# Gates travelling with the rows, result weighting on GpSimd and accumulating gathers in an attention and mixture-of-experts kernel

## The chip, the cores and the metric

The kernel runs on one core of one Trainium2 chip. A core has TensorE (PE; its weight loads are PEld), VectorE (DVE), ScalarE (ACT), GpSimd (POOL) and SyncE (SP), which here only issues DMAs. The metric is the device time of one execution in microseconds (us); lower is better. Each engine works through its own queue in order and waits on semaphores.

## The reference

One layer of a parallel block on x of 32 samples x 256 tokens x 128 features, all float32, cut to what matters:

```python
xn = layernorm(x)
# attention: 16 heads of 64; the first 32 dims of q and k are rotated
q, k, v = xn @ W_qkv;  q, k = rope(q), rope(k)
attn = softmax(causal(q @ k.T) / 8);  a = (attn @ v) @ W_o
# experts: 8 and a ninth that hands its input through, top 2 of 9 by softmax
probs = softmax(xn @ router_w + router_b)
gates = the two largest probs, else 0
y[e] = gelu(xn @ w1[e]) @ w2[e]              # w1: 128x512, w2: 512x128
out = x + a + sum_e gates[e] * y[e] + gates[8] * xn
```

Only the rows that chose an expert are sent through it. Matmuls split float32 into fp16 high and low parts and run three products (`split3`).

## The kernel before, in words

`acc` in SBUF holds x as 64 tiles of 128 tokens and becomes the output. After a prologue (normalisation, transposes, router, and slots: the place of each token's two rows in a list sorted by expert) come three stages.

**Former samples** (0 to 15) and **latter samples** (16 to 31) run the attention, one sample after the other, each in eight *periods* p, one for two heads of the 16. All loops are unrolled in Python, and each engine has its own `sample(b, parity, at)` that writes its queue by hand. Per period, VectorE does: `turned` (some evictions of transposed probabilities), `rest_low`, `masks` (L956: scores plus mask, and row maxima), `turn` (L918, L919: products with cosine and sine of a projected unit), `o_scale` (L983), `invert` in even periods (L966 to L972: reciprocals of the softmax sums in two fp16 parts), `rope_low` (L930), `mix` in period 0 (L907), `combine` in latter samples (L897), `y_add`. TensorE does: `scores` (L1173), `turn_sums` (L1195: the inverses brought into the layout of the outputs; it waits for `inv_parts` of the period before), the projection units of the period (L1102 to L1104), `transposes` (L1184), `attend` (L1211, L1212). ScalarE evicts, does the exponentials (L643), `rest_high` (L587), `v_copy` (L599) and `o_copy` (L633), which takes one of two `o_whole` buffers that GpSimd's `o_split` (L474, L476) frees. GpSimd does `o_split`, `q_rope_low` (L481), `rope_add` (L456, L457) and one indirect DMA a period.

Which unit is projected in which period is laid down by `USUAL`, `AHEAD` and `VALUES`, and `plan` sorts them: within a period `rest` comes last, and in period 6 `v_low`. Units share two PSUM banks in turn.

In former samples GpSimd's `send` (L497) scatters a normalised tile of 128 rows, 512 bytes each, from `stage` to its slots in `sorted_x` in DRAM, twice, for the two choices. `normalise_row` (L488) makes the tile every second period. Each send waits for the landing of the one before (semaphore `sent`):

```python
pool.wait_ge(send_ready, tile + 1)
pool.wait_ge(sent, 16 * (TOP * tile + n))
nc.gpsimd.indirect_dma_start(out=sorted_x, ...in_=stage[:, i, :]...).then_inc(sent, 16)
```

**The experts** stage takes 72 tiles of 256 sorted rows: SP loads (L383) four ahead, TensorE transposes (L1248), computes hidden and down products, ScalarE does gelu (L709), `h_hi` (L714) and the output copy into `ys` (L698), VectorE the fp16 splits (L1062, L1072, L1076), and SP stores to `sorted_y` (L401). GpSimd has nothing to do.

In **latter samples** GpSimd's `gather` (L507) fetches 128 result rows to one of four `stage` buffers, eight a sample (the two tiles of a former sample and the two of this one, two choices each). `combine` (L897) multiplies them by the gate of each token and adds them to `acc`. SP stores finished tiles, and in all samples but the last of a half it copies the parts of q and k into `q_stack` and `k_stack` (L326, four DMAs each, `stack_q` and `stack_k`).

## Time and profile before

| | |
|---|---|
| median of 3 runs | 1500.76 us (1494.09 to 1503.2) |
| profiled execution, time | 1500.74 us |
| profiled execution, span | 1499.0 us |
| busy TensorE / VectorE / ScalarE / GpSimd | 84% / 80% / 75% / 57% |
| mean granted TensorE clock | 0.965 |

The span runs from the first to the last instruction of the profiled execution. Busy shares are means over stages with different limits, so they say little by themselves. In the rows further down, "idle before" and the wait table give the time that an engine stood still and what ended it; L numbers are lines of the kernel.

### The profile page before, as it was taken

Reading aid. Unit: us, or ns where it says so; the run is one execution under the profiler, and the core shown is the slowest. Engines: PE = TensorE matmul, PEld = TensorE weight load, DVE = VectorE, ACT = ScalarE, POOL = GpSimd, SP = SyncE. Lnnn points to the kernel's source line nnn. Section 1 sums busy time; section 2 is a strip of 40 time slices with the busy share of each in tenths; the row PEclk is TensorE's granted clock in tenths of the full one; section 3 lists DMA queues with packets and bytes.
Section 4 is the critical chain, followed back from the end, with each engine's and each line's share of the span. In section 5 each row is a group of like instructions: output and inputs, shape, how many; then the busy total and the mean of one; then the engine's idle time right before and its main releaser. Section 6 shows DMA issues by size and latency. Waiting matters only on the chain.

```text
span 1499.0 us, 46446 instructions
## 1 busy us (share of the span) xinstructions
PE 1254.0 (84%) x15156; PEld 940.5 (63%) x15157; DVE 1195.7 (80%) x4018; ACT 1122.6 (75%) x3606; POOL 858.6 (57%) x1194
## 2 busy tenths in 40 slices
PE   1416999888888898895999999888888889888888
PEld 1404666666666666664889898566666666666666
DVE  5788877777777887783777777889988889889886
ACT  6415888877787787784878887878777777777786
POOL 3254777777777777773000000767777777666775
PEclk9757999999999999997999999999999999999999
DMA  9621433333333333333232322333333333333330
GB/s 290 204 56 38 101 73 73 74 72 72 74 72 74 72 80 79 75 83 111 72 88 84 87 84 75 77 80 79 80 82 92 91 84 80 89 91 89 85 80 27
DMA packets 115831, 130.12 MB, mean 87 GB/s; under 512 B 11568, under 2 KB 75312, under 8 KB 115376
## 3 DMA queue, kind: packets, MB, share of 16 engines
q1 hardware_dynamic: 107056, 110.26, 30.6%
q0 software_dynamic: 8576, 17.33, 3.8%
q8 instruction: 110, 1.80, 0.5%
q14 instruction: 89, 0.73, 0.2%
HBM read 28.85 MB, written 31.59 MB: 40 GB/s over the span
## 4 chain that ended last, share of the span: by engine, by line
PE 28%; DVE 22%; DMA 17%; POOL 16%; issue 13%; ACT 4%; POOLq 0%; DVEq 0%; SPq 0%; ACTq 0%
DMA sorted_x_dram<-stage,slots 17%; PE bank L1102 6%; PE bank L1103 6%; PE bank L1104 6%; DVE arena L956 4%; POOL sorted_x_dram L497 3%; POOL arena L476 3%; PE bank L1173 3%; DVE arena L919 2%; DVE arena L918 2%; POOL arena L456 2%; PE bank L1184 2%; POOL arena L457 2%; ACT probs L643 2%; PE bank L1211 2%
## 5 line engine op out<-in xcount | busy, mean ns | idle before, releaser
L643 ACT ACTIVATE probs<-arena,neg_max 128x128 f32<-128x128 f32 (+1 forms) x1024 | 452.3, 446 | 110.5 <-DVE neg_max L956 108.5
L956 DVE CUSTOM_DVE_ANT_0 arena<-bank,causal 128x128 f32<-128x128 f32 (+1 forms) x1024 | 302.3, 349 | 46.6 <-PE bank L1173 46.1
L507 POOL DMA_INDIRECT stage<-sorted_y_dram,slots x128 | 130.5, 1020 | 257.9 <-DVE arena L919 238.6
L1184 PE MATMUL bank<-ident,probs 128*128 128x128 f32 x1536 | 212.6, 275 | 13.5 <-ACT probsT L626 10.7
L633 ACT ACTIVATE o_whole<-bank 128x256 f32<-128x256 f32 x256 | 97.7, 382 | 151.5 <-PE bank L1195 85.2
L497 POOL DMA_INDIRECT sorted_x_dram<-stage,slots x128 | 133.3, 1041 | 128.6 <-DMA sorted_x_dram<-stage,slots 104.2
L1184 PEld LDWEIGHTS bank<-ident,probs 128*128 128x128 f32 x1536 | 177.2, 142 | 39.6 <-issue 18.4
L643 ACT ACTIVATION_READ_ACCUMULATOR probs<-arena,neg_max 128x1 f32 x1024 | 194.7, 190 | 0.0
L1102 PE MATMUL bank<-arena 128*128 (+1 forms) x864 | 183.2, 238 | 1.5 <-DVE arena L1076 1.5
L476 POOL TENSOR_TENSOR arena<-o_whole,arena 128x256 f16<-128x256 f32 x256 | 172.0, 672 | 21.0
L1103 PE MATMUL bank<-arena 128*128 (+1 forms) x864 | 182.7, 238 | 0.0
L1173 PE MATMUL bank<-arena 64*128 64x128 f16 (+1 forms) x3072 | 172.1, 245 | 12.1 <-DVE neg_max L956 9.8
L1104 PE MATMUL bank<-arena 128*128 (+1 forms) x864 | 178.8, 237 | 0.0
L626 ACT ACTIVATE probsT<-bank 128x384 f32<-128x384 f32 x384 | 170.3, 479 | 2.1
L1195 PE MATMUL bank<-ident_h,inv_parts 128*64 128x128 f16 x2048 | 106.3, 226 | 76.8 <-DVE inv_parts L972 76.5
L1211 PE MATMUL bank<-probsT,arena 128*64 128x256 f32 x1024 | 169.6, 406 | 0.0
L1102 PE MATMUL bank<-xnT_lo,wqk_hi 128*128 128x256 f16 x512 | 142.9, 279 | 27.5 <-DVE arena L924 19.8
L456 POOL TENSOR_TENSOR arena<-arena 128x256 f32<-128x256 f32 x128 | 94.1, 735 | 103.4 <-DVE arena L919 100.7
L1195 PEld LDWEIGHTS bank<-ident_h,inv_parts 128*64 128x64 f16 x2048 | 65.4, 109 | 135.2 <-DVE inv_parts L972 99.6
L924 DVE SCALAR_TENSOR_TENSOR arena<-bank,arena 128x512 f16<-128x512 f32 x128 | 87.5, 685 | 76.4 <-ACT arena L587 76.2
L1104 PE MATMUL bank<-xnT_hi,wqk_hi 128*128 128x256 f16 x512 | 141.3, 276 | 0.0
L1103 PE MATMUL bank<-xnT_hi,wqk_lo 128*128 128x256 f16 x512 | 141.3, 276 | 0.0
(152 smaller groups left out, 3258.8 us busy)
## 6 DMA issues: line engine op xcount, KB each, us to landing
arena<-arena SPq DMA_DIRECT2D x256, 256.0 KB, 3.8
arena<-sorted_x_dram SPq DMA_DIRECT2D x72, 128.0 KB, 2.2
sorted_y_dram<-stage SPq DMA_DIRECT2D x72, 128.0 KB, 1.8
sorted_x_dram<-arena SPq DMA_DIRECT2D x3, 2304.0 KB, 17.8
arena<-experts_dram SPq DMA_DIRECT2D x8, 512.0 KB, 5.6
out_dram<-acc SPq DMA_DIRECT2D x32, 128.0 KB
sorted_x_dram<-arena SPq DMA_DIRECT2D x1, 2368.0 KB, 19.1
sorted_x_dram<-stage,slots POOLq DMA_INDIRECT x128, 2.5
```

The lines of the kernel that those rows point to most:

```text
L476: nc.gpsimd.tensor_tensor(lo, o_whole[:, j % 2, :], hi, ALU.subtract).then_inc(o_done, 1)
L497: nc.gpsimd.indirect_dma_start(out=sorted_x, out_offset=bass.IndirectOffsetOnAxis(ap=slots[:, tile, n:n + 1], axis=0), in_=stage[:, i, :], ...
L626: nc.scalar.activation(probsT[:, s % 4, :], TP[s % 2][:, 0:PW], ACT.Copy).then_inc(t_out[1], 1)
L643: last = nc.scalar.activation(probs[:, s % 4, at:at + w], masked[:, s % 4, at:at + w], ACT.Exp, bias=neg_max[:, s % 4, t:t + 1], scale=-1. ...
L956: last = nc.vector.tensor_tensor_reduce(out=masked[:, (s + i) % 4, at:at + w], in0=SC[i][:, at:at + w], in1=causal[:, at:at + w], scale=1. ...
L1102: mm(dst, a_hi, b_lo, start=start, stop=False)
L1103: mm(dst, a_lo, b_hi, start=False, stop=False)
L1104: return mm(dst, a_hi, b_hi, start=False, stop=stop)
L1173: last = mm(SC[h][:, at:at + w], q_stack[parity][rows, r, ql, u, qs], k_stack[parity][rows, r, kl, u, 0:w], start=(n == 0), stop=(n == 2))
L1184: last = nc.tensor.transpose(TP[s % 2][:, k * P:(k + 1) * P], probs[:, s % 4, k * P:(k + 1) * P], ident[:])
L1195: last = mm(INV[j % 2][64 * i:64 * i + 64, t * P:(t + 1) * P], of, ident_h[:], start=(l == 0), stop=(l == 1))
L1211: mm(PV[j % 2][rows, :], v_sb[:, 0, vs], probsT[:, s % 4, 0:SEQ], start=True, stop=False)
```

## The change

- Rows in DRAM are 129 words wide (`sent_rows`). The last word is the gate of the row for this choice. `stage` holds 2 tiles in place of 4; `normalise_row` therefore waits for the sends of two tiles earlier. GpSimd writes the gate's column before each send.
- In the experts stage GpSimd takes the gate column out of each loaded tile (`keep_gates`) and multiplies the results in `ys` by it (`gate`), before SP stores them. `ys` has buffers of its own. SP's store waits for `gated`.
- Gathers add into `acc` directly (`compute_op=ALU.add`), first both tiles with choice 0, then both with choice 1, each second one waiting for the first of its tile. `combine` is gone from VectorE.
- `o_whole` has three buffers (`OUTPUTS`).
- VectorE's `invert` stands directly behind `masks`.
- In `plan`, units that belong to a sample further ahead come first within a period; nothing is put last any more. In effect `rest` 0 comes before `y` 1 in period 5 and `rest` 1 before `v_low` 1 in period 7.
- ScalarE waits for the last stores of the experts ahead of the first `rest` of the latter samples, since `ys` now lies where the parts of q are.

```diff
+ROW = D + 1
+SENDS = 2
+OUTPUTS = 3
...
-    steps = [(p, kind, j, b if kind == "v_high" else b - 1 if kind == "y" else b + 1)
-             for p, kind, j in (OPENERS if b in (0, MID) else USUAL) if nearer or kind in ("v_high", "y")]
-    steps += [(p, kind, j, b + 2) for p, kind, j in AHEAD if further]
+    opening = b in (0, MID)
+    steps = [(p, kind, j, b + 2) for p, kind, j in AHEAD if further]
+    steps += [(p, kind, j, b if kind == "v_high" else b - 1 if kind == "y" else b + 1)
+              for p, kind, j in (OPENERS if opening else USUAL) if nearer or kind in ("v_high", "y")]
     steps += [(p, kind, j, b + 1) for p, kind, j in VALUES if nearer]
-    return sorted(steps, key=lambda step: (step[0], step[1] == "rest" or step[0] == 6 and step[1] == "v_low"))
+    return sorted(steps, key=lambda step: step[0])
...
-        stage = sb("stage", [P, BACKS, D], F32)
+        stage = sb("stage", [P, SENDS, ROW], F32)
...
-        ys = [stage[:, 2 * i:2 * i + 2, :] for i in range(2)]
+        gate_rows = sb("gate_rows", [P, BODY, 2], F32)
+        ys = [view(PART + i * 256, 256).rearrange("p (k d) -> p k d", d=D) for i in range(2)]
...
                     if not last:
                         sp.wait_ge(xs_ready, i + 1)
+                        sp.wait_ge(gates_kept, i + 1)
                         load(i + BODY, k)
-                    sp.wait_ge(y2_done, i + 1)
+                    sp.wait_ge(gated, i + 1)
...
                 tile = PER * b + i
-                if tile >= PER:
-                    pool.wait_ge(sent, 16 * TOP * (tile - PER + 1))
-                nc.gpsimd.tensor_scalar(stage[:, i, :], acc[:, tile, :], neg_mean[:, tile:tile + 1], rstd[:, tile:tile + 1],
-                                        ALU.add, ALU.mult).then_inc(send_ready, 1)
+                if tile >= SENDS:
+                    pool.wait_ge(sent, 16 * TOP * (tile - SENDS + 1))
+                nc.gpsimd.tensor_scalar(stage[:, i % SENDS, 0:D], acc[:, tile, :], neg_mean[:, tile:tile + 1], rstd[:, tile:tile + 1],
+                                        ALU.add, ALU.mult).then_inc(normalised, 1)
+                nc.gpsimd.tensor_copy(stage[:, i % SENDS, D:ROW], gates[:, tile, 0:1]).then_inc(send_ready, 1)
 
             def send(b, k):
 
                 i, n = k // TOP, k % TOP
                 tile = PER * b + i
-                pool.wait_ge(send_ready, tile + 1)
                 pool.wait_ge(sent, 16 * (TOP * tile + n))
+                if n > 0:
+                    nc.gpsimd.tensor_copy(stage[:, i % SENDS, D:ROW], gates[:, tile, n:n + 1]).then_inc(send_ready, 1)
+                pool.wait_ge(send_ready, TOP * tile + n + 1)
+                pool.wait_ge(normalised, tile + 1)
                 nc.gpsimd.indirect_dma_start(
...
+            def keep_gates(i, k):
+
+                pool.wait_ge(xs_in[k], 4 * (i - k) + 16)
+                if i >= BODY:
+                    pool.wait_ge(gated, i - BODY + 1)
+                nc.gpsimd.tensor_copy(gate_rows[:, k, :], xs[k][:, :, D]).then_inc(gates_kept, 1)
+
+            def gate(i, k):
+
+                pool.wait_ge(y2_done, i + 1)
+                pool.wait_ge(gates_kept, i + 1)
+                for j in range(ET // P):
+                    last = nc.gpsimd.tensor_scalar(ys[k % 2][:, j, :], ys[k % 2][:, j, :], gate_rows[:, k, j:j + 1], 1.0, ALU.mult, ALU.mult)
+                last.then_inc(gated, 1)
+
             def gather(b, k):
...
-                if not (u == 0 and k < BACKS):
-                    pool.wait_ge(combined, TOP * PER * u + k - BACKS + 1)
+                t, n = BACK[k % 4]
+                tile = (TPS * u if k < 4 else TPS * b) + t
+                if n > 0:
+                    pool.wait_ge(gathered[t], 32 * u + 16 * (k // 4) + 16)
+                elif k >= 4:
+                    pool.wait_ge(mixed, b + 1)
                 nc.gpsimd.indirect_dma_start(
-                    out=stage[:, k % BACKS, :], out_offset=None, in_=sorted_y[0:ROWS, :],
+                    out=acc[:, tile, :], out_offset=None, in_=sorted_y[0:ROWS, :], compute_op=ALU.add,
...
+            for i in range(2):
+                keep_gates(i, i)
+            for i in range(TILES):
+                if i + 2 < TILES:
+                    keep_gates(i + 2, (i + 2) % BODY)
+                gate(i, i % BODY)
             for done in ys_out:
...
-                if not (isinstance(J, int) and J < 2):
-                    act.wait_ge(o_done, J - 1)
-                nc.scalar.activation(o_whole[:, j % 2, :], PV[j % 2], ACT.Copy).then_inc(o_out, 1)
+                if J >= OUTPUTS:
+                    act.wait_ge(o_done, J - OUTPUTS + 1)
+                nc.scalar.activation(o_whole[:, J % OUTPUTS, :], PV[j % 2], ACT.Copy).then_inc(o_out, 1)
...
+                    if at == REOPEN and p == 0:
+                        for done in ys_out:
+                            act.wait_ge(done, 16 * TILES // 2)
...
                     masks(b, 2 * p)
+                    then = past(b, p, 2)
+                    if then and p % 2 == 0:
+                        invert(4 * then[0] + then[1] // 2, then[1] // 2)
                     for kind, j, of, u, psum in units_at(b, p):
                         if kind == "rope":
                             turn(j, u, psum, of)
                     then = past(b, p, INV_LAG)
                     if then:
                         o_scale(8 * then[0] + then[1], then[1])
-                    then = past(b, p, 2)
-                    if then and p % 2 == 0:
-                        invert(4 * then[0] + then[1] // 2, then[1] // 2)
...
-                    then = past(b, p, BACK_LAG)
-                    if then and b >= MID:
-                        combine(*then)
```

## Rows read from the trace of the kernel before

**Rows 1.** The page: busy us (share of the span) and instructions of each engine.
```profile
PE 1254.0 (84%) x15156; PEld 940.5 (63%) x15157; DVE 1195.7 (80%) x4018; ACT 1122.6 (75%) x3606; POOL 858.6 (57%) x1194
```
**Rows 2.** By stretch: length, PE, PEld, DVE, ACT, POOL busy, clock, DMA, GB/s.
```profile
158.13:653.10 494.97, 440.22 (x5329) 313.69 (x5329) 388.28 (x1484) 389.70 (x1343) 373.18 (x530) 1.00 0.34 77
720.00:920.00 200.00, 195.45 (x2490) 179.45 (x2488) 146.23 (x262) 163.27 (x328) 0.00 (x0) 1.00 0.30 87
968.45:1427.95 459.50, 407.46 (x4951) 290.51 (x4950) 411.99 (x1482) 361.48 (x1249) 322.93 (x443) 1.00 0.36 85
```
**Rows 3.** Waits, former samples (158 to 653): waiter, awaited: us, times, longest.
```profile
POOL sorted_x_dram L497 <- DMA sorted_x_dram<-stage,slots: 88.5, 44, 3.2
...
PE bank L1195 <- DVE inv_parts L972: 31.7, 29, 3.5
...
POOL sorted_x_dram L497 <- POOL stage L488: 14.7, 40, 0.7
```
**Rows 4.** Chain that ended last, former sample: start us, us, what.
```profile
524.51 4.99 DMA sorted_x_dram<-stage,slots
...
529.52 0.02 POOLq L496
529.54 0.73 issue
530.27 4.38 DMA sorted_x_dram<-stage,slots
```
**Rows 5.** Waits, latter samples (968 to 1428).
```profile
POOL arena L456 <- DVE arena L919: 70.8, 38, 3.2
...
PE bank L1195 <- DVE inv_parts L972: 38.7, 39, 1.2
DVE arena L924 <- ACT arena L587: 31.9, 27, 1.7
...
PE bank L1102 <- DVE arena L924: 10.9, 13, 0.8
```
**Rows 6.** Groups by line, VectorE, latter samples (968.45 to 1427.95).
```profile
L897 DVE SCALAR_TENSOR_TENSOR acc<-stage,gates,acc 128x128 f32<-128x128 f32 x104 | 52.1, 501 | 0.0
...
L918 DVE TENSOR_TENSOR arena<-bank,arena 128x512 f32<-128x512 f32 x52 | 35.5, 683 | 0.0
...
L930 DVE TENSOR_TENSOR arena<-arena 128x512 f16<-128x512 f32 x26 | 23.5, 905 | 0.0
```
**Rows 7.** Groups by line and form, GpSimd, the whole span.
```profile
L507 POOL DMA_INDIRECT stage<-sorted_y_dram,slots x128 | 130.5, 1020 | 257.9 <-DVE arena L919 238.6 <-issue 8.3 <-DVE acc L897 1.7
...
L488 POOL TENSOR_SCALAR stage<-acc,neg_mean,rstd 128x128 f32<-128x128 f32 x64 | 28.4, 444 | 24.3 <-DVE small L881 24.3
...
L425 POOL MEMSET rank<- 128x1 f32 x9 | 0.4, 181 | 0.0
```
**Rows 8.** DMA issues: count, KB each, median us to landing.
```profile
stage<-sorted_y_dram,slots POOLq DMA_INDIRECT x128, 2.6
```
**Rows 9.** Timeline of GpSimd in one former sample, periods 7, 0, 4, 6.
```profile
511.42 1.01 POOL L497 DMA_INDIRECT sorted_x_dram<-stage,slots  x1 [0.15 <-issue]
...
515.42 1.03 POOL L497 DMA_INDIRECT sorted_x_dram<-stage,slots  x1 [0.28 <-POOL stage L488]
...
535.41 1.03 POOL L497 DMA_INDIRECT sorted_x_dram<-stage,slots  x1 [2.25 <-DMA sorted_x_dram<-stage,slots]
...
542.62 1.04 POOL L497 DMA_INDIRECT sorted_x_dram<-stage,slots  x1 [0.45 <-POOL stage L488]
```
**Rows 10.** Timeline of SP's queue beside it (523 to 536).
```profile
523.87 11.04 SPq L326 DMA_DIRECT2D arena<-arena  x8
```
**Rows 11.** Groups by line, VectorE, experts (720 to 920).
```profile
L1076 DVE TENSOR_TENSOR arena<-arena 128x512 f16<-128x512 f32 x132 | 91.4, 693 | 13.6 <-ACT arena L714 11.4
...
L1072 DVE CAST arena<-arena 128x512 f16<-128x512 f32 x65 | 27.8, 427 | 20.9 <-ACT arena L709 20.1
L1062 DVE TENSOR_TENSOR arena<-bank,arena 128x256 f16<-128x256 f32 x65 | 27.6, 425 | 19.2 <-ACT arena L691 10.6 <-PE bank L1104 6.4
```

75 lines of the change are left out of this document (32 added, 43 removed).

## The prediction

> **What bounds the kernel now.** The page comes first: four engines busy for 57% to 84% of the span [rows 1], so no engine fills it and the stages have to be read apart. The busy table [rows 2] is cut at the first masks of samples 1, 15, 17 and 30. Fourteen former samples take 494.97 us, 35.36 each; thirteen latter ones 459.50, 35.35 each. The pace is the same, the limits are not. The granted clock is 1.00 in all stretches and plays no part.
>
> *Former samples.* The wait table [rows 3] has GpSimd waiting 88.5 us for its own earlier scatter to land and 14.7 for its own normalise_row, and for no other engine. Busy 373.18 [rows 2] and these waits make 476 of 495 us; the rest is dispatch between them. The chain [rows 4] agrees: scatter, landing, sequencer step, next scatter. GpSimd sets the pace. TensorE's 31.7 us of waiting for inv_parts is time it would lose elsewhere.
>
> *Experts.* TensorE is busy 195.45 of 200 us and GpSimd not at all [rows 2].
>
> *Latter samples.* GpSimd waits 70.8 us for VectorE in rope_add alone [rows 5], so it has room. VectorE is busy 411.99 of 459.50 us, 31.7 a sample; TensorE 407.46, 31.3 [rows 2]. TensorE's idle time is 4.0 us a sample, of which 38.7/13 = 3.0 waits for inv_parts and 10.9/13 = 0.8 for rest_low [rows 5]. The two engines take turns in holding each other.
>
> **The change, part by part.** The sum is made against the profiled execution, span 1499.0 and time 1500.74, which is the median of the three runs (1500.76) to 0.02 us.
>
> *Latter: combine goes.* 104 L897 at 501 ns, 52.1 us in 13 samples [rows 6]: 4.0 us of VectorE a sample. *Inversion behind masks.* Today two turns of 0.68 [rows 6] and an o_scale stand between masks and invert, and TensorE finds inv_parts late 39 times by 1.0 us on average [rows 5]. With invert some 1.6 us earlier all of these waits go. Invert needs the last exponentials of the period before; they end while masks runs, which is the cover of its wait. If ScalarE came later, the turns behind invert would be late by as much. *Unit order.* rest ahead of y and v_low brings rest_high forward by one v_copy, about 0.5 us; VectorE waits 31.9 us for it and TensorE 10.9 behind that [rows 5].
>
> With VectorE at 31.7 - 4.0 = 27.7, TensorE's 31.3 us is the floor. I walked one sample through both queues with these durations. In period 0 VectorE still has rest_low 0.6, masks 1.35, invert 0.9, two turns 1.2, o_scale 0.35 and mix 1.1, together 5.5 us, against 31.3/8 = 3.9 of TensorE, which then stops about 0.5 us at a bank that waits for rest_low. Smaller stops in periods 3, 6 and 7 add 0.8. So 31.3 + 1.3 = 32.6 us, a gain of 2.75. Fourteen steady samples give 38.5, the first and last ones 2.5: **-41**. Bounds: all of the 4.0 us goes in 15 samples, -60; only the stops behind rest_low go, 0.8 each, -13.
>
> *Gathers that add.* No row shows an adding transfer. The plain gather holds GpSimd 1.02 us [rows 7] and lands in 2.6 [rows 8]. The second gather of a row waits for the first, which was issued two periods, 8 us, before. Bounds: 2.6 us as now, or twice that for a second stream; either is hidden. GpSimd's own part: 1.0 to 2.0 us, and 2.0 adds 8 us to 322.93/13 = 24.8 busy [rows 2], about the new pace. By the nearest row, the plain gather, I take no cost.
>
> *Former: the gate column.* Each sample gains eight one-column copies. The nearest row is a memset of one column, 181 ns, nine of them overlapped into 0.4 us [rows 7]. More is in where the waits stand. A wait that is a sequencer step of its own (POOLq L496) is followed by 0.73 us before the scatter starts [rows 4]; the wait that the scatter carries, for normalise_row, costs 0.28 [rows 9]. In today's code send_ready is named first and is the carried one. Afterwards sent comes first for the first send of a row, and send_ready becomes the step. So that scatter goes from 0.28 to 0.1 + 0.73 behind normalise_row: +0.55 in periods 0 and 2, +0.4 in period 6 (0.45 now), and -0.5 in period 4, whose landing wait (2.25 now) becomes the carried one [rows 9]. A second send adds 0.18 for the copy and 0.28 for its wait, less today's dispatch of 0.15 [rows 9]: +0.3 in periods 1 and 7, and nothing in 3 and 5, where landing, copy and carried wait make what landing and 0.73 make now. Sum +1.6. Scatters land in 5.0 and 4.4 us beside the eight stack transfers [rows 4, 10]; rows of 516 for 512 bytes may add 0 to 0.2 us to four landings, and period 2's delay is partly absorbed by that queue. I take **+1.7 a sample, 15 samples, +25.5**. Bounds: copies overlapped and carried waits a gain, 0; every copy with 0.18 and 0.28 and the steps besides, 4.0 a sample, +60. Third buffer, early inversion and unit order relieve ScalarE, VectorE and TensorE, none of which sets the pace here: 0. The stage of two rows asks for a landing two sends back, past by then: 0.
>
> *Experts.* GpSimd gets two multiplications of 128x128 (0.44 us by L488 [rows 7]) and a small copy a tile, 1.1 of 2.9 us, between ScalarE's output and SP's store. The buffer is wanted again two tiles, 5.7 us, later; 0.4 + 1.1 and a landing, at 2.6 as for the gather [rows 8], fit. SP's load of four tiles ahead, queued behind that store, moves by 1.1 us and is not late. Taken +1; bounds 0 and rival 4. At the change to the latter samples GpSimd and ScalarE wait for the stores, 1 us later: +1. The zero fill grows by 1% (129 for 128 words) and is waited for in sample 0 only: 0.
>
> Sum: 1500.7 - 41 + 25.5 + 2 = **1487 us**.
>
> **A rule against the change.** First the row: VectorE's L930 averages 905 ns in the latter samples, beside GpSimd's work [rows 6], for as many elements as L1076's 693 beside an idle GpSimd [rows 11]. The Trainium skill, "SBUF — State Buffer", on the doors to it, says that VectorE and GpSimd share a port pair which one instruction locks while the other blocks. By that the multiplications would stop L1072 and L1076 in the experts and the sum would be rival 4's 1505; by the averages over the stretch it stays 1487.
>
> **The rivals.**
> 1. *The gate column is free*: 1500.7 - 41 + 2 = 1462. For it: the copies are tiny. Against: GpSimd has no slack to hide them in [rows 3].
> 2. *The gate column decides*: at 4.0 us a sample 1500.7 - 41 + 60 + 2 = 1522. From (41 - 2)/15 = 2.6 us a sample on the kernel is slower than before. For it: every scatter waits for a fresh copy. Against: a send that waits for a landing anyway, as in period 4 [rows 9], hides most of it.
> 3. *The latter gain is small*, because adding gathers hold GpSimd or period 0 of VectorE holds TensorE: 1500.7 - 13 + 25.5 + 2 = 1515.
> 4. *VectorE loses in the experts*: its queue there is 693 + 693 + 427 + 425 ns [rows 11], with two stops of 0.44 added 3.1 us against 2.87 a tile, +0.25 x 72 = 18: 1505. Against: 0.8 us a tile is idle.
>
> **How the numbers follow.** Forecast 0.42, rival 1 0.18, rival 2 0.14, rival 3 0.16, rival 4 0.10. About 1%, 15 us, is what a measurement of this kernel can tell from no change. The forecast's own range is 1474 to 1500; one per cent under the old time is 1485.7, near its middle, so 0.22 of its 0.42 count as faster and 0.20 as the same. Faster: 0.22 + 0.18 = 0.40. Same: 0.20 + 0.08 of rival 4 + 0.04 of rival 3 + 0.02 of rival 2 = 0.34. Slower: the rest, 0.26. Leaving out a tenth on either side: 1460 to 1520.
>
> **What would show it.** Right: former samples near 37.1 us with GpSimd waiting for nobody else and about 0.8 us ahead of first sends; latter samples near 32.6, L1195's wait for inv_parts gone, TensorE over 95% busy; experts unchanged. Wrong: former samples at 35.4 or under, or GpSimd waiting for VectorE there; gathers landing in over 8 us; L1076 over 0.9 us in the experts.

## The result, and the profile after

| | before | after |
|---|---|---|
| median of the runs, us | 1495.47 (1491.22 to 1503.2) | 1506.49 (1501.93 to 1510.12) |
| profiled execution, us | 1500.74 | 1506.63 |
| its span, us | 1499.0 | 1504.9 |
| samples 1 to 14, us each | 35.36 | 36.78 |
| samples 17 to 29, us each | 35.35 | 34.15 |

The ratio after to before is 1.0066, 95% interval 1.005 to 1.0081: the kernel became slower by 0.7%, some 10 us, and not 14 us faster. That is clear of noise, but under the 1% below which the prediction counted a time as the same. The 1487 us of the forecast are missed; the time lies within its range of 1460 to 1520.

The span can be cut at the first masks of the same samples as [rows 2]. From before to after: prologue 127.1 to 128.4 us, samples 0 to 14 526.0 to 546.8, sample 15 with the experts 281.5 to 283.6, sample 16 33.8 to 34.0, samples 17 to 29 459.5 to 443.9, the end 71.0 to 68.1. That is +1.3 + 20.8 + 2.1 + 0.2 - 15.6 - 2.9 = +5.9 us, the difference of the two spans.

The page's busy line of the kernel after (compare [rows 1]):

```profile
PE 1278.5 (85%) x15156; PEld 961.5 (64%) x15157; DVE 1138.7 (76%) x3890; ACT 1123.1 (75%) x3606; POOL 1010.8 (67%) x1538
```

VectorE lost 57 us of work and GpSimd gained 152, and TensorE, whose instructions are the same, is busy 24.5 us longer. The busy table by stretch (length, then PE, PEld, DVE, ACT, POOL, granted clock, DMA share, GB/s; compare [rows 2]):

```profile
160.31:675.20 514.89, 453.41 (x5324) 323.02 (x5325) 375.57 (x1485) 391.46 (x1342) 384.43 (x642) 0.97 0.32 75
740.00:940.00 200.00, 195.12 (x2472) 178.30 (x2470) 144.80 (x260) 161.69 (x325) 57.52 (x195) 1.00 0.31 85
992.82:1436.75 443.93, 415.63 (x4944) 300.69 (x4946) 374.98 (x1378) 359.19 (x1247) 382.64 (x441) 0.97 0.45 88
```

In the last row GpSimd has gone from 322.93 to 382.64 us in a stretch that is shorter. The granted clock of the first and last row has fallen from 1.00 to 0.97: stretches at the 1.2 GHz level are now among those at 2.4.

Groups by line in the latter samples of the kernel after (the adding gather is L539; before, L507 took 1020 ns [rows 7]):

```profile
L539 POOL DMA_INDIRECT acc<-sorted_y_dram,slots x104 | 166.5, 1601 | 22.3 <-issue 7.6 <-DMA acc<-sorted_y_dram,slots 7.5
L484 POOL CAST arena<-o_whole 128x256 f16<-128x256 f32 x104 | 80.9, 777 | 0.0
...
L465 POOL TENSOR_TENSOR arena<-arena 128x256 f32<-128x256 f32 x52 | 46.3, 891 | 30.6 <-DVE arena L947 30.6
...
L935 DVE TENSOR_SCALAR acc<-acc,small 128x128 f32<-128x128 f32 x26 | 30.6, 1215 | 0.0
```

The adding gather holds GpSimd 0.58 us longer, 8 times a sample. The L484 behind it starts in the record 1.00 us after the gather's start, while the gather still runs, and so is shown longer than it is. GpSimd's idle time ahead of rope_add (L465) has gone from 70.8 us [rows 5] to 30.6. VectorE's mix (L935) takes 1215 ns; before it was L907:

```profile
L907 DVE TENSOR_SCALAR acc<-acc,small 128x128 f32<-128x128 f32 x26 | 15.9, 652 | 0.0
```

Waits of the same stretch (compare [rows 5]):

```profile
PE bank L1124 <- DVE arena L952: 25.9, 12, 2.3
...
POOL acc L539 <- DMA acc<-sorted_y_dram,slots: 7.5, 5, 1.7
```

TensorE's waits for inv_parts (38.7 us before) are gone, as forecast. In their place it waits twelve times in thirteen samples, 2.2 us each, for rest_low in period 0. The second line is new too: in period 6 of five samples GpSimd stands 1.3 to 1.7 us until the adding gather of period 4 has landed, 6.7 to 7.1 us after its issue. This did not make the samples longer: one of the five takes 32.3 us, four 33.7 to 33.8, and the eight without this wait 34.5 to 34.7.

The timeline of one of TensorE's stops, first VectorE, then GpSimd, then TensorE (start us, us, engine, line; in brackets the idle time before it):

```profile
1199.10 1.08 DVE L1000 SCALAR_TENSOR_TENSOR inv_parts<-inv_total,inv_parts 128x8 f16<-128x8 f32 x1
...
1201.63 2.12 DVE L935 TENSOR_SCALAR acc<-acc,small 128x128 f32<-128x128 f32 x2
1203.67 0.68 DVE L952 SCALAR_TENSOR_TENSOR arena<-bank,arena 128x512 f16<-128x512 f32 x1
```
```profile
1199.00 1.16 POOL L491 TENSOR_TENSOR arena<-arena 128x512 f16<-128x512 f32 x1
1200.30 1.58 POOL L539 DMA_INDIRECT acc<-sorted_y_dram,slots  x1
1201.52 1.13 POOL L465 TENSOR_TENSOR arena<-arena 128x256 f32<-128x256 f32 x1
1202.21 1.12 POOL L466 TENSOR_TENSOR arena<-arena 128x256 f32<-128x256 f32 x1
```
```profile
1204.40 0.39 PE L1124 MATMUL bank<-xnT_lo,wqk_hi 128*128 128x256 f16 x1 [2.14 <-DVE arena L952]
```

Mix (two operations, one line here) starts at 1201.63, while the gather still runs to 1201.88. Its first operation lasts 1.79 us, to 1203.42, just behind the second rope_add operation (L466), which ends at 1203.33; its second takes 0.41. Rest_low (L952) waits behind mix, and TensorE stands 2.14 us. The busy table of the 3.5 us ahead of the stop, of the 3.4 us behind it and of what follows has the granted clock at 1.00, 0.52 and 1.00:

```profile
1198.80:1202.26 3.46, 3.46 (x43) 2.33 (x40) 3.43 (x6) 3.11 (x12) 3.31 (x5) 1.00 0.10 12
1204.40:1207.80 3.40, 3.40 (x16) 2.53 (x18) 3.08 (x12) 2.87 (x11) 2.58 (x4) 0.52 0.18 24
1207.80:1212.00 4.20, 4.20 (x51) 2.82 (x49) 3.18 (x15) 3.52 (x13) 3.97 (x5) 1.00 0.07 10
```

Behind the stop TensorE runs at the 1.2 GHz level: its products of 256 columns start 0.21 us apart (timeline, 1204.59 to 1205.45), where they had started 0.11 us apart ahead of it.

In the former samples GpSimd still waits for its own work, but for 3.8 us in fourteen samples that the profile puts down to VectorE (waits, 160 to 675; L500 and L508 are the gate copies; compare [rows 3]):

```profile
POOL sent_rows_dram L511 <- DMA sent_rows_dram<-stage,slots: 34.5, 18, 3.3
POOL stage L508 <- DMA sent_rows_dram<-stage,slots: 28.9, 33, 1.6
POOL sent_rows_dram L511 <- POOL stage L500: 28.5, 37, 0.8
POOL sent_rows_dram L511 <- POOL stage L508: 21.3, 46, 0.9
POOL sent_rows_dram L511 <- DVE arena L947: 3.8, 10, 1.0
```

And the chain that ended last, through one first send of a row (compare [rows 4]; POOLq is GpSimd's sequencer, L510 the wait for normalised):

```profile
386.27 0.43 POOL stage L498
386.70 0.15 POOL stage L500
386.85 0.03 POOLq L510
386.88 0.52 issue
387.40 0.02 POOLq L463
387.41 0.19 issue
387.61 1.05 POOL sent_rows_dram L511
```

### The profile page after: what moved, and what is told of

Read it like the earlier page. It is cut to its first block, busy times and chain, and to the rows that moved or that the text cites. A ratio compares the mean times of both kernels' runs of the same rounds, so it can differ in the third digit from the quotient of the medians.

```text
span 1504.9 us, 46790 instructions
## 1 busy us (share of the span) xinstructions
PE 1278.5 (85%) x15156; PEld 961.5 (64%) x15157; DVE 1138.7 (76%) x3890; ACT 1123.1 (75%) x3606; POOL 1010.8 (67%) x1538
## 3 DMA queue, kind: packets, MB, share of 16 engines
q0 software_dynamic: 22912, 17.40, 6.8%
HBM read 28.92 MB, written 31.73 MB: 40 GB/s over the span
## 4 chain that ended last, share of the span: by engine, by line
PE 41%; POOL 24%; DVE 13%; issue 11%; DMA 8%; ACT 3%; POOLq 0%; DVEq 0%; SPq 0%; ACTq 0%
PE bank L1124 8%; PE bank L1125 8%; PE bank L1126 7%; DMA sent_rows_dram<-stage,slots 7%; POOL sent_rows_dram L511 6%; PE bank L1206 5%; PE bank L1233 4%; PE bank L1195 4%; POOL arena L486 4%; POOL arena L465 3%; POOL arena L466 3%; POOL arena L491 2%; POOL arena L484 2%; PE bank L1217 2%; DVE arena L984 2%
## 5 line engine op out<-in xcount | busy, mean ns | idle before, releaser
L1206 PE MATMUL bank<-ident,probs 128*128 128x128 f32 x1536 | 223.2, 284 | 9.6 <-ACT probsT L664 8.3
L539 POOL DMA_INDIRECT acc<-sorted_y_dram,slots x128 | 204.5, 1598 | 29.9 <-issue 9.7
L1206 PEld LDWEIGHTS bank<-ident,probs 128*128 128x128 f32 x1536 | 185.1, 147 | 43.7 <-issue 20.7
L511 POOL DMA_INDIRECT sent_rows_dram<-stage,slots x128 | 132.1, 1032 | 106.9 <-DMA sent_rows_dram<-stage,slots 42.6
L486 POOL TENSOR_TENSOR arena<-o_whole,arena 128x256 f16<-128x256 f32 x256 | 178.3, 696 | 21.0
L1233 PE MATMUL bank<-probsT,arena 128*64 128x256 f32 x1024 | 174.6, 417 | 0.0
L527 POOL TENSOR_SCALAR arena<-arena,gate_rows 128x128 f32<-128x128 f32 x144 | 54.4, 389 | 173.4 <-ACT arena L739 173.4
L484 POOL CAST arena<-o_whole 128x256 f16<-128x256 f32 x256 | 152.4, 595 | 3.0 <-DVE o_whole L1012 2.5
L465 POOL TENSOR_TENSOR arena<-arena 128x256 f32<-128x256 f32 x128 | 105.7, 826 | 59.5 <-DVE arena L947 57.6
L1195 PEld LDWEIGHTS bank<-arena 64*128 64x128 f16 x3072 | 98.5, 95 | 63.4 <-issue 49.1
```

The source lines that it names most:

```text
L484: nc.gpsimd.tensor_copy(hi, whole).then_inc(o_hi, 1)
L486: nc.gpsimd.tensor_tensor(lo, whole, hi, ALU.subtract).then_inc(o_done, 1)
L511: nc.gpsimd.indirect_dma_start(out=sent_rows, out_offset=bass.IndirectOffsetOnAxis(ap=slots[:, tile, n:n + 1], axis=0), in_=stage[:, i % S ...
L539: nc.gpsimd.indirect_dma_start(out=acc[:, tile, :], out_offset=None, in_=sorted_y[0:ROWS, :], compute_op=ALU.add, in_offset=bass.IndirectO ...
L1195: last = mm(SC[h][:, at:at + w], q_stack[parity][rows, r, ql, u, qs], k_stack[parity][rows, r, kl, u, 0:w], start=(n == 0), stop=(n == 2))
L1206: last = nc.tensor.transpose(TP[s % 2][:, k * P:(k + 1) * P], probs[:, s % 4, k * P:(k + 1) * P], ident[:])
```

## The experiments

Seventeen kernels, in the order of the argument and not of the runs. Each ratio is against the kernel before, run beside it on the same chip; that of the kernel after is 1.0066. "Former" and "latter" are the lengths of samples 1 to 14 and 17 to 29 in the profiled execution.

| kernel | ratio, 95% interval | former | latter |
|---|---|---|---|
| before | 1 | 35.36 | 35.35 |
| after | 1.0066 (1.005 to 1.0081) | 36.78 | 34.15 |
| e4_sched_only | 0.9826 (0.9789 to 0.9862) | 35.44 | 33.42 |
| e2_plain_gather | 0.9827 (0.9801 to 0.9853) | 36.51 | 32.06 |
| e5_plain_busy | 0.9956 (0.994 to 0.9971) | 36.78 | 32.73 |
| e10_plain_busy2 | 0.9912 (0.9879 to 0.9945) | 36.80 | 32.47 |
| e15_plain_busy3 | 0.9941 (0.992 to 0.9963) | 37.10 | 32.69 |
| e16_plain_busy4 | 0.9916 (0.9897 to 0.9935) | 37.06 | 32.87 |
| e13_gather_behind | 1.0035 (1.0014 to 1.0055) | 36.70 | 34.44 |
| e1_mix_p3 | 0.9935 (0.9913 to 0.9957) | 36.96 | 33.41 |
| e3_wait_order | 1.0073 (1.0048 to 1.0098) | 37.28 | 34.55 |
| e6_copy_first | 1.0079 (1.0052 to 1.0105) | 37.01 | 33.88 |
| e9_norm_first | 1.0026 (1.0004 to 1.0047) | 36.17 | 33.88 |
| e14_rows_only | 0.9918 (0.9889 to 0.9947) | 35.70 | 34.48 |
| e11_after_qall | 0.9835 (0.9808 to 0.9861) | 35.05 | 33.02 |
| e12_after_norm_mix_qall | 0.9696 (0.9668 to 0.9724) | 35.12 | 31.73 |
| e7_sched_qlow | 0.9694 (0.9659 to 0.973) | 33.98 | 33.16 |
| e8_sched_mix_qlow | 0.963 (0.96 to 0.9661) | 33.56 | 32.22 |
| e17_sched_mix_qall | 0.9669 (0.9645 to 0.9693) | 33.87 | 33.22 |

How far a profile's former samples vary of themselves can be read here: eight of the kernels (after and the seven with changes in the latter samples only) have the same code there and lie between 36.51 and 37.10.

### The schedule alone

In the kernel before, with everything else left as it is there:

```diff
                     masks(b, 2 * p)
+                    then = past(b, p, 2)
+                    if then and p % 2 == 0:
+                        invert(4 * then[0] + then[1] // 2, then[1] // 2)
...
-    return sorted(steps, key=lambda step: (step[0], step[1] == "rest" or step[0] == 6 and step[1] == "v_low"))
+    return sorted(steps, key=lambda step: step[0])
```

> The kernel before with two of the edits alone: invert directly behind masks, and the new unit order. No gates in rows, no adding gathers, two output buffers. If GpSimd alone sets the former pace: former samples within 0.3 us of 35.36. Theory 1: mix and combine now follow the turns directly and run against rope_add in the latter samples; mix averages over 900 ns (652 before), the wait of TensorE for inv_parts goes (38.7 us), but the latter samples gain at most 1.5 us of 35.35. Rival: they gain 2.5 us or more, ratio 0.97 to 0.98.

Measured 0.9826 of before: early inversion and unit order, two parts of the change, are worth 26 us by themselves. The latter samples fall by 1.9 us with combine still on VectorE, TensorE's waits for inv_parts are gone from the list, and the former samples stay (35.44), as they would if GpSimd sets their pace. Of the two theories neither was met: mix stays at 0.7 us an operation (theory 1 had 0.9), and the gain of 1.9 us a sample lies between the 1.5 of theory 1 and the 2.5 of its rival. The third output buffer was not tried alone.

### Adding or plain gathers

```diff
-   out=acc[:, tile, :], out_offset=None, in_=sorted_y[0:ROWS, :], compute_op=ALU.add,
+   out=acc[:, tile, :], out_offset=None, in_=sorted_y[0:ROWS, :],
```

> The changed kernel with gathers that overwrite the output rows instead of adding to them; what is left out is the addition, so rows of the output lose x and the other choice. Theory 1 (mix against rope_add): GpSimd's issue falls from 1.60 to 1.02 us, but latter samples stay within 0.4 us of 34.15; ratio 1.00 to 1.007. Theory 2 (the adding gather is what costs the latter gain): latter samples fall to about 32.6 us, ratio 0.985 to 0.99. Theory 3 (contention by the adding transfers' many packets): stack transfers back to 3.8 us from 5.1 and latter samples under 33.5.

The whole loss of the latter samples hangs on the addition: 32.06 us each and 0.9827 of before. Rows of the groups by line and of the waits, latter samples:

```profile
L539 POOL DMA_INDIRECT acc<-sorted_y_dram,slots x104 | 105.9, 1019 | 15.6 <-issue 6.0
...
POOL arena L465 <- DVE arena L947: 73.6, 52, 4.0
```

A plain gather in the new place takes what it took before, 1.02 us, and GpSimd's idle time ahead of rope_add is back. The prediction's walk gave 32.6 us for exactly this kernel. Theory 3, that the many packets of adding gathers slow SP's stack transfers and these the samples, is not borne out: they land in 3.7 us here and in 5.1 in the kernel after, but in 3.8 in e13 below, whose latter samples are as long as those of the kernel after.

Is it GpSimd's longer issue or the transfer? Four kernels kept the plain gather and put an operation on the stage, with a wait for it, ahead of each:

```diff
+   nc.gpsimd.memset(stage[:], 0.0).then_inc(spare, 1)
+   pool.wait_ge(spare, 8 * u + k + 1)
```

That is the first. In place of the memset the second and third have a tensor_scalar over 160 and 250 words of the stage, the fourth a tensor_tensor over 176.

> The changed kernel with plain gathers (the addition is left out, the gathered row overwrites the output row), and one memset of the 258-word stage and a wait for it ahead of each of the 120 gathers: about 0.6 us more of GpSimd a gather, as the adding gather costs over the plain one (1.60 for 1.02 us), but with the plain transfer's packets. Theory A, GpSimd's own longer issue is what the latter samples lose: they come out near 34.1 us each as in the changed kernel, 1479 + 30 = 1509 us at most, 1500 at least. Theory B, the adding transfers themselves (144 packets for 32) slow the others: latter samples stay near 32.1 us, 1480 us.

> As the plain-busy run (plain gathers that overwrite the output row, the addition is left out), but with a tensor_scalar over 160 words of the stage and a wait for it ahead of each gather in place of the memset: about 0.60 us more of GpSimd a gather than the plain gather has, as much as the adding gather takes over it (the memset added about 0.43). Theory A, GpSimd's time is what the latter samples lose, and it costs steeply once GpSimd's slack ends: 33.8 to 34.3 us a latter sample, 1500 to 1507 us. Theory B, half or more of it is the adding transfer itself: 32.7 to 33.1 us, 1488 to 1494.

> As the second plain-busy run, with 250 words in place of 160: about 0.60 us more of GpSimd a gather than a plain gather takes (the 160 words added about 0.44), which is what the adding gather takes over the plain one. The gathers are plain and overwrite the output row, the addition is left out. Theory A, GpSimd's time alone makes the loss, by sliding its operations onto VectorE's mix or past the o_split that TensorE waits for once its slack is used up: 33.6 to 34.4 us a latter sample, 1497 to 1508 us. Theory B, the rest is in the adding transfers themselves: 32.5 to 33.1 us, 1484 to 1492 us, and mix's first operation stays near 0.71.

> Plain gathers that overwrite the output row (the addition is left out), and ahead of each a subtraction over 176 words of the stage with a wait for it, some 0.1 us longer than the last dose. GpSimd's time outside its waits for VectorE was 31.1 us a latter sample with the last dose and 31.8 in the changed kernel; here it should be 31.7 to 32.1. Theory A, GpSimd's time alone makes the loss, steeply at the end of its slack: mix's first operation 1.7 us or more, or TensorE waiting for o_split, 33.6 to 34.4 us a latter sample, 1497 to 1508 us. Theory B, the rest is in the adding transfers: 32.7 to 33.1 us, mix's first operation 0.71, 1487 to 1493 us.

GpSimd's time per sample outside its idle time ahead of rope_add (length of a sample less 1/13 of that row) was, from the plain kernel over the four doses to the kernel after: 26.4, 29.0, 30.1, 31.1, 31.4 and 31.8 us. The samples took 32.06, 32.73, 32.47, 32.69, 32.87 and 34.15. So 5.0 us more of GpSimd with plain transfers cost 0.8 us, and the kernel after, 0.4 further on, costs 1.3 more. Those 0.4 are not work: the waits for landings make 7.5/13 = 0.6 us of the 31.8, and 1.3/13 = 0.1 of the 31.4 of the fourth dose. Without them the two have 31.2 and 31.3 us. So the fourth dose fell short of the 31.7 to 32.1 that it aimed at, yet it gives GpSimd as much work as the kernel after has. Theory B came nearer in all four; theory A, that GpSimd's time costs steeply, was not seen. What did not happen in these four is the stop of TensorE. Of idle gaps of TensorE over 1.5 us they have none in the latter samples; the kernel after has twelve, 25.9 us in all, and its TensorE is busy 415.63/13 = 31.97 us a sample, against 404.81/13 = 31.14 in e16 (busy table, the same samples):

```profile
993.99:1421.27 427.28, 404.81 (x4947) 292.32 (x4948) 367.28 (x1379) 357.39 (x1246) 369.54 (x545) 1.00 0.38 91
```

That is 0.83 of the 1.28 us between the two kernels, for the same products at a granted clock of 0.97 for 1.00; the rest is idle time.

In e16, at the same place of a sample, the gather is over before mix begins:

```profile
1193.70 0.98 POOL L542 DMA_INDIRECT acc<-sorted_y_dram,slots  x1 [0.27 <-POOL stage L540]
1194.80 0.73 POOL L465 TENSOR_TENSOR arena<-arena 128x256 f32<-128x256 f32 x1
1195.49 0.73 POOL L466 TENSOR_TENSOR arena<-arena 128x256 f32<-128x256 f32 x1
```
```profile
1194.91 1.39 DVE L938 TENSOR_SCALAR acc<-acc,small 128x128 f32<-128x128 f32 x2
```

The gather ends at 1194.68, 0.23 us ahead of mix, rope_add is under way when mix begins, and mix takes 1.39 us for its two operations, and 2.12 in the kernel after. There the gather ends 0.25 us after mix has begun; the record of rope_add (1201.52) starts ahead of mix there too, but it is 1.13 us long in place of 0.73 and overlaps the gather. The traces split cleanly by this place: where the gather ends 0.04 to 0.25 us behind mix's start (twelve samples of the kernel after, and as many of e3 and of e14), mix's first operation takes 1.78 to 1.93 us; where it ends 0.2 us or more ahead of it (the thirteenth sample, e2, and all four doses), it takes 0.70 to 0.71. In one sample of e6 (26) mix's first operation runs wholly beside the gather, and takes 0.33 us: so the gather itself does not hold it, but what follows it.

### Moving the collision

```diff
-                    else:
+                    elif p > 0:
                         gather(b, p)
                     for kind, j, of, u, psum in units_at(b, p):
                         if kind == "rope":
                             rope_add(j, of)
+                    if b >= MID and p == 0:
+                        gather(b, p)
```

> The changed kernel with the gather of period 0 issued behind rope_add instead of ahead of it. GpSimd's work is the same; only its place against VectorE's mix in period 0 moves: the two products of rope_add start as soon as turn is done, not 0.3 us behind mix's start. Theory A, the latter samples lose by that collision (the first of mix's two operations takes 1.78 us in the changed kernel and 0.71 with plain gathers, and TensorE stands 2.1 us behind it): the first falls to about 0.7, period 0 from 6.84 to 5.6 or 5.8 us, latter samples from 34.15 to 32.9 to 33.2 us, 1488 to 1493 us. Theory B, GpSimd's longer gathers hold the latter samples wherever they stand: 33.9 to 34.4 us, 1503 to 1510.

The collision did go, as theory A had it: the first operation of mix averages 706 ns (1775 in the kernel after) and period 0 falls from 6.84 to 5.78 us. But period 4 rose from 3.87 to 6.32, and the sample is not shorter (34.44; the five kernels with the latter code of the kernel after lie between 33.88 and 34.55). TensorE now stops as often for another partner (waits, 1010 to 1430, TensorE):

```profile
PE bank L1126 <- POOL arena L486: 24.4, 12, 2.0
PE bank L1126 <- DVE arena L954: 12.2, 12, 1.4
```

Theory A was right on period 0 and wrong on the sample, theory B right on the sample to 0.04 us: with adding gathers GpSimd is late somewhere in nearly every sample, here with the split of the output rows (L486) that the y unit needs. Mix moved away from period 0 says the same:

```diff
-                    if p == 0:
+                    if p == 3:
                         if b >= MID:
                             mix(b)
```

> The changed kernel with mix moved from period 0 to period 3 of each sample, where GpSimd has no rope_add. Theory 1 (in the changed kernel mix, now directly behind the turns, runs against GpSimd's rope_add and stands still: its two instructions take 2.66 us of period 0 and TensorE waits 2.1 us): mix averages under 700 ns in the latter samples instead of 1215, period 0 falls from 6.9 to about 5.0 us, latter samples from 34.15 to 32.3 us, no clock dips there, ratio to the kernel before 0.985 to 0.99. Theory 2 (the adding gather's 1.6 us of GpSimd delays rope_add, and mix is long only because it waits for nothing better): latter samples stay above 34 us, ratio 1.00 to 1.007. Theory 3 (landings contend: stack transfers 5.1 us): as theory 2.

33.41 us, 0.5 under the lowest of those five. Theory 1's period 0 came (4.70 for 5.0), its 32.3 us did not; again TensorE waits for L486 (waits, 990 to 1407):

```profile
PE bank L1124 <- POOL arena L486: 20.8, 11, 2.0
```

### What the gate column costs

A wait counts as fresh here when the operation just ahead of the scatter is what satisfies it; it is either carried by the scatter or a sequencer step of its own.

```diff
+                if n == 0:
+                    pool.wait_ge(send_ready, TOP * tile + 1)
                 pool.wait_ge(sent, 16 * (TOP * tile + n))
```

> The changed kernel with one edit in send: for a tile's first choice the wait for send_ready is named ahead of the wait for sent, so that the scatter carries it. If the placing of waits costs what the prediction says: the idle time ahead of first sends falls from 0.77 to 0.28 us in periods 0, 2 and 6 and grows by 0.5 in period 4, so former samples fall by about 1.0 us from 36.78, 15 us in all, ratio 0.995 to 1.00. Rival (the copies themselves and the landings set the pace, the placing does not): former samples within 0.3 us of 36.78, ratio as before, 1.005 to 1.008.

37.28 us a former sample, above what either theory allowed. This edit was badly aimed: send_ready became the carried wait, but the third wait, for normalised, stayed a sequencer step and was nearly as fresh. The gap ahead of the first send went from 0.77 to 0.67 us only. The next also missed:

```diff
+                nc.gpsimd.tensor_copy(stage[:, i % SENDS, D:ROW], gates[:, tile, 0:1]).then_inc(send_ready, 1)
                 nc.gpsimd.tensor_scalar(stage[:, i % SENDS, 0:D], acc[:, tile, :], neg_mean[:, tile:tile + 1], rstd[:, tile:tile + 1],
                                         ALU.add, ALU.mult).then_inc(normalised, 1)
-                nc.gpsimd.tensor_copy(stage[:, i % SENDS, D:ROW], gates[:, tile, 0:1]).then_inc(send_ready, 1)
```

> The changed kernel with the first gate's copy ahead of normalise_row's tensor_scalar. Theory A, the preparation of a scatter (about 0.72 us) begins when the instruction ahead of it is dispatched and is covered by it: the 0.44 us tensor_scalar covers it again where the 0.18 us copy did not, the gap ahead of first sends in periods 0, 2 and 6 falls from 0.77 to 0.28 us, former samples gain 1.0 to 1.4 us (36.8 to about 35.6), 1486 to 1492 us. Theory B, the two copies, the two waits and the longer rows cost what the samples lose: under 0.3 us a sample, 1502 to 1506.

No gain, and a gap of 0.81 us behind an operation of 0.44. That refutes its theory A, that the operation ahead covers the scatter's preparation. In both kernels a wait step follows the last operation. So the third edit kept the copy first and named normalised first:

```diff
+                if n == 0:
+                    pool.wait_ge(normalised, tile + 1)
+                    pool.wait_ge(send_ready, TOP * tile + 1)
                 pool.wait_ge(sent, 16 * (TOP * tile + n))
```

> The changed kernel with the first gate's copy ahead of normalise_row's tensor_scalar, as in the copy-first run, and the first send naming its waits in another order: normalised first, then send_ready, then sent. Theory A, a scatter carries the wait that is named first and the others are sequencer steps; 0.73 us pass between the last step and the scatter, 0.28 behind a carried wait. In the copy-first run normalised was still a step and the gap stayed 0.81. Here the only fresh wait is carried: the gap ahead of first sends in periods 0, 2 and 6 falls to 0.3 to 0.4 us, former samples gain 1.0 to 1.4 us (36.8 to about 35.6), 1486 to 1492 us. Theory B, the steps' place makes no difference: the gap stays 0.8, 1505 us. Theory C, the gap falls but a landing behind it takes the time back: gap 0.3, former samples over 36.5.

Timelines of GpSimd in a period 2, e6 first, then e9:

```profile
384.58 0.44 POOL L499 TENSOR_SCALAR stage<-acc,neg_mean,rstd 128x128 f32<-128x128 f32 x1
385.83 1.05 POOL L511 DMA_INDIRECT sent_rows_dram<-stage,slots  x1 [0.81 <-POOL stage L499]
```
```profile
383.15 0.48 POOL L499 TENSOR_SCALAR stage<-acc,neg_mean,rstd 128x128 f32<-128x128 f32 x1
383.94 1.05 POOL L514 DMA_INDIRECT sent_rows_dram<-stage,slots  x1 [0.30 <-POOL stage L499]
```

The gap falls to 0.30 us here, and to 0.34, 0.34 and 0.40 as medians of periods 0, 2 and 6: what decides is whether the fresh wait is carried by the scatter or is a step before it. The former samples fall to 36.17, 0.6 us less than in the kernel after and outside the 36.51 to 37.10 of the unchanged code, but not the 1.0 to 1.4 expected. Three gaps, each from 0.77, give 1.2; in period 4, where the scatter waits for a landing, the landing's wait has become the step, and 0.8 us pass from it to the scatter, not 0.27. That leaves 0.7, near the 0.6 measured. The time is 1.0026 of before.

```diff
+            nc.gpsimd.memset(stage[:, :, D:ROW], 0.25).then_inc(send_ready, 1)
...
-                nc.gpsimd.tensor_copy(stage[:, i % SENDS, D:ROW], gates[:, tile, 0:1]).then_inc(send_ready, 1)
...
-                if n > 0:
-                    nc.gpsimd.tensor_copy(stage[:, i % SENDS, D:ROW], gates[:, tile, n:n + 1]).then_inc(send_ready, 1)
-                pool.wait_ge(send_ready, TOP * tile + n + 1)
                 pool.wait_ge(normalised, tile + 1)
+                pool.wait_ge(sent, 16 * (TOP * tile + n))
```

> The changed kernel without the copies of the gates: the 129th column of the stage is set once, to 0.25, so that every result is weighted by 0.25 and not by its gate; rows of 516 bytes and the rest of the change stay, and a scatter waits for normalised (named first) and sent, as in the kernel before. Theory A, the copies and their waits are the whole loss of the former samples: 36.78 back to 35.3 to 35.5 us, 1484 to 1487 us. Theory B, the longer rows (their landings) are a part, what was left in the norm-first run: 36.0 to 36.2 us, 1494 to 1497.

35.70 us a former sample, and 0.9918 of before. By the ratios 1.5% or 22 us lie between this kernel and the kernel after, about what the former samples had lost (20.8 us); by the profiles it is 1.1 of the 1.42 us a sample. So the copies with their waits are most of it, at the least. The 35.70 lie between the two theories: 0.3 us above the kernel before, no more than the spread of such profiles, so a small part for the rows of 516 bytes is neither shown nor excluded. One effect of these rows is plain, in the DMA issues by form (count, KB each, median us to landing), before and then after:

```profile
sorted_x_dram<-arena SPq DMA_DIRECT2D x3, 2304.0 KB, 17.8
```
```profile
sent_rows_dram<-arena SPq DMA_DIRECT2D x3, 2322.0 KB, 37.7
```

The zero fill takes twice as long. It lies in the prologue, but does not set its length: the five kernels with the old fill (before, e4, e7, e8, e17) have prologues of 127.1 to 128.4 us, those with the new one 126.9 to 128.9.

### Giving GpSimd room

```diff
-                        if kind == "rope" and j < 2:
+                        if kind == "rope" and j < 0:
                             q_rope_low(j, of)
...
-                        if kind == "rope" and j >= 2:
+                        if kind == "rope" and j >= 0:
                             rope_low(j, of)
```

> The changed kernel with the lower half of the turned q blocks made by VectorE, not GpSimd, in all samples: 2.3 us a sample off GpSimd, 1 to 2 us on VectorE. Theory A, GpSimd's time is the limit in the former samples and its lateness that of the latter: former 36.8 to about 34.5 to 35.5, latter 34.15 to 32.3 to 33.2, together 1455 to 1475 us. Theory B, the latter samples are held by VectorE's period 0 alone, which only gets more work: latter 34.2 to 35, former down all the same, 1475 to 1490 us.

Both parts of theory A hold: former 35.05 and latter 33.02, 0.9835 of before, 35 us less than the kernel after's ratio gives, for 2.3 us of work a sample moved from GpSimd to VectorE. Only four gaps over 1.5 us are left in TensorE, again behind rest_low, though mix's first operation takes no more than 0.75 us there; their cause stays open. The nine samples without one take 32.4 to 32.7 us, the four with one 33.6 to 34.9. With the two other repairs:

> The changed kernel with all three repairs: normalised as the carried wait, mix in period 3, the lower half of q by VectorE in all samples. If the three causes add: former samples 33.5 to 34, latter 32.0 to 32.5, 1438 to 1450 us, level with the kernel before with early inversion, new unit order and the same two moves (1439). If the adding gathers cost by themselves, beyond GpSimd's time: latter samples 33 or more, 1455 or more.

31.73 us a latter sample, less than with plain gathers and mix in period 0, and no gap over 1.5 us. So with room on GpSimd adding gathers cost little: TensorE is busy 31.1 of these 31.7 us, which leaves at most 0.6 for them and everything else. The same kernel with plain gathers was not run. The forecast of 1438 to 1450 was missed by the former samples: 35.12 us, not 34, no better than without the order of waits (35.05).

The same moves on the kernel before, with early inversion and new unit order but without gate column and adding gathers, the first with q in the former samples only and mix where it was, the second with mix in period 3, the third with all of q as well:

> The kernel before with the early inversion and the new unit order, and in the former samples the lower half of the two turned q blocks is made by VectorE, not GpSimd. Theory A, GpSimd sets the pace of the former samples (busy plus the landings of its own scatters): 2.3 us of work a sample taken off it bring them from 35.4 to 33.1 to 34.0 us, 1479 - 15 x 1.5 to 2.2 = 1446 to 1457 us. Theory B, TensorE or the scatters' landings hold them: 35.0 to 35.4 us, 1474 to 1480.

> As the kernel before it in this series (early inversion, new unit order, lower half of q by VectorE in former samples), and mix moved from period 0 to period 3. Theory A, the pile of VectorE's work in period 0 holds TensorE in the latter samples: 33.4 falls to about 32.6 us, 12 us less than without it. Theory B, TensorE's pace is set elsewhere: within 3 us of it, as period 4 loses what period 0 gains.

> The kernel before with the early inversion, the new unit order, mix in period 3, and the lower half of q by VectorE in all samples, not in the former ones alone (1439 us). Theory A, the combine operations (4.5 us of VectorE a latter sample) hold what is left there: with 2 us more on VectorE the latter samples go from 32.2 to 32.6 or more, 1444 us or more. Theory B, VectorE has room and GpSimd does not: 31.8 us, 1433 us.

Ratios 0.9694, 0.963 and 0.9669; the second took 1438.96 us (1435.14 to 1443.92). The first shows directly that GpSimd sets the pace of the former samples: 2.3 us of work less, 1.5 us a sample less. The second is the fastest kernel of the study, 3.7% under the kernel before and 4.3% under the kernel after. Mix in period 3 is worth 0.9 us a latter sample, as expected. The third is on theory A's side: with combine on VectorE the latter samples cannot take q too, 33.22. Against e12, which differs from it in the change's remaining parts and the order of waits, it can be read what these parts are worth once GpSimd has room: the latter samples gain 1.5 us, the former lose 1.25, and the ratios (0.9696 and 0.9669) do not differ.

## Why the prediction was wrong, point by point

*Bounds before.* Right for both stages. e7 shows GpSimd's pace in the former samples, e4 that TensorE and VectorE had held each other in the latter.

*Latter samples, combine, inversion and unit order, -2.75 a sample.* Right in mechanism and in size, for the kernel that was walked through: with plain gathers it is 32.06, 3.3 us under before, 0.5 better than the walk. The walk's period 0 (mix 1.1 us, TensorE stopping 0.5) fits e2, where mix takes 1.4 and the period 5.2.

*Adding gathers at no cost.* This is the step that failed. The prediction gave bounds of 1.0 to 2.0 us for GpSimd's part of one and said that 2.0 would bring GpSimd about to the new pace. Then it took the plain gather as the nearest row and booked nothing. The measured 1.60 us makes 4.6 us a sample. The cost came to 2.1 us a sample, 28 us between the spans of e2 (1476.6) and of the kernel after, and 36 us by the two ratios. Of the 2.1 us, 0.8 go with GpSimd's longer time as such (e16) and 1.3 with TensorE's stops and the clock behind them; it is why the latter samples gained 18 us in place of 41. That a landing is hidden failed as well, in five samples of thirteen: it took 6.7 to 7.1 us, beyond the bound of twice 2.6, and GpSimd was ready for the second gather 5.7 us after the first, not 8; but these waits did not make the samples longer. With plain gathers (e2) the rest of the forecast would have been too low, 26 us of gain by the ratio against 14. Had the middle of the bounds been taken, 4 us more of GpSimd a sample, the question would have been what GpSimd is late for, and TensorE waits for its output rows.

*Clock.* "Plays no part" held for before only. Behind the stop shown above TensorE runs at the lower level for 3.4 us, and TensorE's busy time in the latter samples is 31.97 - 31.34 = 0.6 us a sample above before [rows 2].

*Former samples, gate column, +1.7 a sample.* Measured +1.42, and +20.8 us against 25.5 for 15 samples. The mechanism (carried wait 0.28, step 0.73) held: 0.77 us ahead of the first send in periods 0, 2 and 6 (forecast 0.8), 0.27 in period 4. Two experiments seemed to speak against it and were wrongly aimed; e9 confirmed it. The bounds of 0 to 4 us a sample were far too wide.

*Experts and change to the latter samples, +2.* Sample 15 with the experts +2.1, sample 16 +0.2. VectorE's L1098 and L1094 (before, L1076 and L1072 [rows 11]) take 692 and 427 ns, as before.

*Zero fill at 0.* Booked as 1% more bytes; its landing doubled. The 0 held all the same, since the prologue varies as much between kernels with the same fill. The +1.3 us between the two profiles are within that.

*The rule against the change.* It was weighed for the wrong stage. The Trainium skill, "SBUF — State Buffer", on the two sides of SBUF, says that of a VectorE instruction with two inputs in SBUF and a GpSimd one that reads SBUF, whichever starts first has the shared port pair for its whole length and the other waits. The experts show nothing of it. In period 0 of the latter samples the trace agrees for one operation: the timeline above has VectorE's L1000, which has two such inputs, at 1.08 us (0.26 on average), begun 0.1 us behind GpSimd's L491 and ending with it. Mix has only one such tensor as input, and its first operation stands through both operations of rope_add and not only one; by that sentence of the Trainium skill it does not follow. That the port is what holds mix was not tested by itself.

*The rivals.* Rival 3 is what happened in the latter samples: the gain there is 18 us (15.6 and 2.9 less 0.2; the 2.9 are the end, which lies between 68.1 and 71.4 in the five kernels with this code) against its 13, and its reason, adding gathers that hold GpSimd together with period 0 that holds TensorE, was right in both halves. With the rest as forecast it gave 1515; the measured differences made it 1506. It had 0.16. Rivals 1 and 2 would have needed former samples at 35.4 or 39.4, rival 4 slower experts; none is seen. Each stage by itself was within its bounds, and so the time within the range, which was wide enough for a loss and a gain alike; the sum came out on the other side of zero because the two largest terms, -41 and +25.5, have opposite signs.

## What stays open

As much GpSimd time with plain transfers cost 0.8 of the 2.1 us. The remaining 1.3 go with TensorE's stops and the clock behind them, which every kernel with adding gathers and q on GpSimd had (e1, e3, e6, e9, e13, e14 and the kernel after: twelve each) and no kernel with plain gathers. Why the gather of period 0 ends behind mix's start in the one and 0.2 us ahead of it in the others, at the same work, was not separated: it may be the late landings, or the transfers (an adding gather makes 144 packets where a plain one makes 32, by the queue's total of 22912 for 8576). Nor was it tested whether a plain gather that ends behind mix's start would bring the stops too.

## What to carry to other kernels

Work that is taken off one engine and given to a queue is still someone's time: price the new instruction on the engine that issues it at the middle of its bounds, not at the nearest row, and ask which of that engine's other results comes late. Once the sum of two large terms of opposite sign is smaller than either one's uncertainty, test the parts apart: here the two edits of the schedule held a gain of 1.7% (e4), and the rest cost more than it brought. Name first the wait that will end last; here a wait step behind the last operation cost 0.4 to 0.5 us a transfer.

## What the runs showed of the hardware that was not expected

An indirect gather that adds holds GpSimd 1.60 us against 1.02 for 128 rows of 512 bytes. Waits for semaphores ahead of an indirect transfer are not alike: from a fresh wait step to the scatter 0.73 us pass (kernel after, e6), behind a carried wait 0.28 to 0.40 (before, e9, e14), and the length of the operation ahead hardly matters (gaps of 0.77 behind 0.18 us, 0.81 behind 0.44). The first operation of mix on VectorE lasts 1.78 to 1.93 us when it starts 0.04 to 0.25 us before an adding gather on GpSimd ends and rope_add's two operations follow without a gap, 0.70 to 0.71 when it starts 0.1 us behind the first of these two (e2 and the doses), and 0.33 wholly beside a gather (e6, once). An adding gather issued in period 4 took 6.7 to 7.1 us to land in the five samples where GpSimd waited for it. Filling DRAM with rows of 516 instead of 512 bytes took 33.4 to 38.0 us in the fourteen kernels that have them, against 17.8 in the other five.
